# Post-norm decoder layer with experts on one core: the experts' second bias as one float32r product of split rows, the gate weights split by GpSimd

## The reference, cut to what matters

```
def _moe(h, w_gate, we1, be1, we2, be2):      # h: 2048 tokens x 256, E = 4 experts, I = 256
    raw = softmax(x @ w_gate, axis=-1)
    top_vals, top_idx = top_k(raw, 2)
    w = softmax(top_vals, axis=-1)
    comb = zeros((t, E)).at[arange(t)[:, None], top_idx].add(w)
    hmid = gelu(einsum('td,edi->tei', x, we1) + be1[None], approximate=False)
    eout = einsum('tei,eid->ted', hmid, we2) + be2[None]
    out = einsum('te,ted->td', comb, eout)
```

## Time and profile before

| | us |
|---|---|
| median of 3 runs | 1181.89 (1181.88 to 1181.89) |
| the profiled execution, its time | 1185.99 |
| its span | 1184.2 |
| what lies around the span | 1.79 |
| granted TensorE clock, mean | 0.985 of full speed |

### The profile page before, as it was taken

How to read it: one execution, slowest core, us unless ns; L and a number is a source line. 1 busy time by engine, 2 the same in 40 slices (tenths; PEclk the granted TensorE clock), 3 DMA queues, 4 the chain that set the end, 5 groups by cost and what they waited for, 6 DMA issues and landing times.

```text
span 1184.2 us, 30629 instructions
## 1 busy us (share of the span) xinstructions
PE 1116.1 (94%) x11732; PEld 921.1 (78%) x11732; DVE 954.0 (81%) x2219; ACT 667.3 (56%) x1703; POOL 660.2 (56%) x714
## 2 busy tenths in 40 slices
PE   6899999899999999888999999999999999999997
PEld 5667665566666766556899899999999899988887
DVE  6758886877888878867788888888898888878977
ACT  5466564577777777664555544444444444558663
POOL 4457564654545556264778554544544455737665
PEclk9889999989999999989999999999999999999999
DMA  5975544344444444402121000000000100101111
GB/s 162 211 183 131 130 122 110 99 122 120 120 135 135 117 126 119 121 22 86 58 72 55 2 1 1 1 1 1 1 1 1 37 2 1 37 19 36 37 37 36
DMA packets 107490, 83.05 MB, mean 70 GB/s; under 512 B 74171, under 2 KB 95803, under 8 KB 107345
## 3 DMA queue, kind: packets, MB, share of 16 engines
q1 hardware_dynamic: 107345, 81.10, 25.0%
HBM read 57.02 MB, written 23.07 MB: 68 GB/s over the span
## 4 chain that ended last, share of the span: by engine, by line
PE 55%; DVE 14%; issue 6%; POOL 4%; ACT 2%; SPq 1%; DMA 1%; POOLq 0%; DVEq 0%; ACTq 0%
PE bank L1637 5%; PE bank L1638 5%; PE bank L1639 5%; PE bank L1693 4%; PE bank L1666 4%; PE bank L665 3%; PE bank L643 3%; PE bank L562 3%; PE bank L1653 2%; PE bank L1708 2%; PE bank L1706 2%; PE bank L1707 2%; DVE B_nr L808 2%; PE bank L1654 2%; PE bank L1655 2%
## 5 line engine op out<-in xcount | busy, mean ns | idle before, releaser
L1941 POOL TENSOR_TENSOR C_QK<-C_t1b,C_t2b 128x512 f32<-128x512 f32 x128 | 168.7, 1318 | 227.4 <-DVE C_t2b L1780 226.8
L1777 DVE SCALAR_TENSOR_TENSOR C_t1b<-bank,C_bcol,C_tabs 64x512 f32<-64x512 f32 x256 | 192.1, 750 | 38.6 <-PE bank L1639 34.5
L1067 ACT ACTIVATE PT<-bank 128x512 f32<-128x512 f32 x224 | 130.0, 596 | 98.5 <-PE bank L643 96.7
L808 DVE TENSOR_REDUCE B_nr<-bank 128x4 f32<-128x512 f32 x256 | 164.2, 683 | 25.4 <-PE bank L604 25.1
L1637 PE MATMUL bank<-C_XTh,C_Wh 128*128 128x512 f32 x256 | 112.4, 439 | 5.7 <-DVE C_XTl L1626 1.9
L1873 ACT ACTIVATE C_P<-bank,C_nm 128x128 f32<-128x128 f32 x256 | 90.5, 366 | 34.1 <-DVE C_nm L1790 32.4
L1892 ACT ACTIVATE C_V<-bank 128x512 f32<-128x512 f32 x64 | 38.0, 596 | 124.1 <-PE bank L1655 122.6
L1638 PE MATMUL bank<-C_XTl,C_Wh 128*128 128x512 f32 x256 | 101.6, 397 | 0.0
L1639 PE MATMUL bank<-C_XTh,C_Wl 128*128 128x512 f32 x256 | 101.2, 395 | 0.0
L665 PE MATMUL bank<-PT,vpool 128*32 128x128 f32 x2048 | 97.6, 287 | 2.0 <-ACT OTf L1077 2.0
L1780 DVE SCALAR_TENSOR_TENSOR C_t2b<-bank,C_bcol,C_tabs 128x512 f32<-128x512 f32 x128 | 96.1, 751 | 1.8
(11 more groups left out here) (271 smaller groups left out, 3495.0 us busy)
## 6 DMA issues: line engine op xcount, KB each, us to landing
Adrq<-PB SPq DMA_DIRECT2D x16, 192.0 KB, 2.9
Adrk<-PB SPq DMA_DIRECT2D x16, 192.0 KB, 3.1
stk<-Adrq SPq DMA_DIRECT2D x16, 192.0 KB
stk<-Adrk SPq DMA_DIRECT2D x16, 192.0 KB
Bdrq<-PB SPq DMA_DIRECT2D x16, 192.0 KB, 3.0
stk<-Bdrq SPq DMA_DIRECT2D x32, 96.0 KB
Bdrk<-PB SPq DMA_DIRECT2D x16, 192.0 KB, 2.8
stk<-Bdrk SPq DMA_DIRECT2D x32, 96.0 KB
```

The costliest lines, as they stand in the source:

```text
L808: e.tensor_reduce(dst, bank[n % 2][:, :].rearrange("p (a b) -> p a b", a=4), AX.X, ALU.max, negate=True).then_inc(sem("m_dve"), 1)
L1067: e.activation(pt_of(n)[:, :], bank2(n)[:, :], ACT.Exp).then_inc(sem("e_act"), 1)
L1777: e.scalar_tensor_tensor(out=v4(t1b[kq][lo:lo + 64, :]), in0=v4(o[hi:hi + 64, :]), scalar=bc[hi:hi + 64, :], in1=tabsC[hi:hi + 64, 2 * kq ...
L1941: e.tensor_tensor(QK[v % 3][:, kq, :], t1b[kq][:, :], t2b[kq][:, :], ALU.add).then_inc(sem("rc_pool"), 1)
```

## The change

The bias product becomes a float32r product. To keep its precision the operands are split, and the parts lie at different partitions of the same product: in comb128 the columns 0 to 15 and 16 to 31 (through a view of two runs of 64, k = 2, of which the first 16 columns are taken: columns 0 to 15 and 64 to 79) get the weights as float32r, and columns 32 to 47 get what is left of them. In b2, three copies of the rows lie at partitions 0, 32 and 64. ScalarE copies b2 to the float32r tile b2r once (bias_act), and VectorE subtracts that from b2 in partitions 64 to 95 once (bias_dve), so that these hold the low part. One product then sums high x high (partitions 0 on), low weights x high bias (32 on) and high weights x low bias (64 on).

GpSimd does the splitting of the weights (comb_pool): it zeroes the tile in the first two chunks, copies the weights twice as float32r, and subtracts. It stands ahead of residual(0, 0) for chunk 0, and ahead of the last part's hidden_pool (m = 7) for chunks 1 to 3. VectorE writes the weights into a tile of their own (D_combS); its zeroing instruction goes. TensorE's transposition now waits for GpSimd's semaphore comb_zero, and no longer for VectorE's gate_dve.

```diff
+    b2r = sb("D_b2r", [128, 4, 256], F32R, st_d)
...
-    comb = [T[:, 0:16].rearrange("p (a b) -> p a b", a=4) for T in comb128]
-    combT = [sb(f"D_combT{i}", [128, 128], F32, st_d) for i in range(2)]
+    comb = [sb(f"D_combS{i}", [128, 4, 4], F32, st_d) for i in range(2)]
+    combT = [sb(f"D_combT{i}", [128, 128], F32R, st_d) for i in range(2)]
...
     def comb_t_pe(e, q, c):
-        q.wait_ge("gate_dve", 18 * (c + 1))
+        q.wait_ge("comb_zero", min(c, 1) + 1 + 2 * (c + 1))
...
-            q.wait_ge("ld_b2", 16)
+            q.wait_ge("ld_b2", 18)
...
-                    e.matmul(ebank(c, b, x)[:, 256:512], combT[i][:, :], b2[:, b, :], start=True, stop=True)
+                    e.matmul(ebank(c, b, x)[:, 256:512], combT[i][:, :], b2r[:, b, :], start=True, stop=True)
...
-            if c < 2:
-                e.memset(comb128[c][:, :], 0.0).then_inc(sem("comb_zero"), 1)
...
-            q.wait_ge("comb_zero", min(c, 1) + 1)
+            if c >= 2:
+                q.wait_ge("comb_zero", 2 + 2 * (c - 1))
...
+        bias_dve(e, q)
         for c in range(1, NCH):
...
+    def bias_act(e, q):
+        q.wait_ge("ld_b2", 16)
+        e.activation(b2r[:, :, :], b2[:, :, :], ACT.Copy).then_inc(sem("ld_b2"), 1)
+
+    def bias_dve(e, q):
+        low = slice(64, 96)
+        q.wait_ge("ld_b2", 17)
+        e.tensor_tensor(b2r[low, :, :], b2[low, :, :], b2r[low, :, :].bitcast(F32), ALU.subtract).then_inc(sem("ld_b2"), 1)
+
+    def comb_pool(e, q, c):
+        T = comb128[c % 2]
+        if c < 2:
+            e.memset(T[:, :], 0.0).then_inc(sem("comb_zero"), 1)
+        n = min(c, 1) + 1 + 2 * c
+        flat = comb[c % 2][:, :, :].rearrange("p a b -> p (a b)")
+        copies = T[:, :].rearrange("p (k r) -> p k r", k=2)[:, :, 0:16].bitcast(F32R)
+        q.wait_ge("comb_zero", n)
+        q.wait_ge("gate_dve", 18 * (c + 1))
+        if c >= 2:
+            q.wait_ge("ct_pe", c - 1)
+        e.tensor_copy(copies, flat.unsqueeze(1).to_broadcast([128, 2, 16])).then_inc(sem("comb_zero"), 1)
+        q.wait_ge("comb_zero", n + 1)
+        e.tensor_tensor(T[:, 32:48], flat, T[:, 0:16], ALU.subtract).then_inc(sem("comb_zero"), 1)
...
     def act_d(e):
         q = Queue(e, sem)
+        bias_act(e, q)
...
         LAST = (3, 5, 6, 7)
+        comb_pool(e, q, 0)
         residual(0, 0)
         for c in range(1, NCH):
             for m in range(8):
...
+                if m == 7:
+                    comb_pool(e, q, c)
                 hidden_pool(e, q, c, m)
...
     for b in range(4):
-        f["Db2"][4 * b:4 * b + 4, b, :] = g("be2").reshape(4, 256)
+        for k in range(3):
+            f["Db2"][32 * k + 4 * b:32 * k + 4 * b + 4, b, :] = g("be2").reshape(4, 256)
```

## The result

The changed kernel takes 1189.34 us (median of 6 runs, 1187.66 to 1192.03); the kernel before, run beside it, 1181.89 us (6 runs, 1180.90 to 1183.80). The ratio is 1.0057, 95% interval 1.0039 to 1.0074: slower by some 6.7 us (4.6 to 8.7). The forecast was 1186.0 (4.15 us slower), in a range from 1183.8 to 1188.2. The direction came true and the time lies outside the range. The profiled execution took 1190.62, its span 1188.8 us, with a mean granted clock of 0.984.

What follows compares the result with a forecast made beforehand. VectorE was taken to set the pace from 1086.53 to about 1135, TensorE from 1137.17 to 1150.24, then VectorE, then a chain begun by GpSimd. 2.9 + 1.65 - 0.6 + 0.2 = 4.15 us on 1181.89 gave 1186.0, range 1183.8 to 1188.2.

Steps and rivals of the forecast that it cites:

- the first stall: Chunk 0's transposition waits for GpSimd's three splitting instructions and starts at 1086.35; TensorE has nothing to do for 3.9 us.
- the price at full clock: VectorE's first L2201 starts at 1089.45 instead of 1086.53, 2.9 us late, if TensorE's clock stays up.
- TensorE's saving: Sixteen bias products each 0.31 us cheaper, 5.0 us in all; only 0.6 counts, from chunk 2's first two.
- the 3.09 of the forecast: Time in us from chunk 0's transposition to VectorE's L2201: 3.74 less a 0.34 wait and 0.31 of cheaper bias product.
- the rival on the faster side: VectorE's two-operand gate instructions run free of GpSimd in 3 chunks, giving 6.6 us: 1179.4, chance 0.05.
- the prediction's signs of being wrong: L2201 starting before 1089, VectorE gaps between there and 1140, or TensorE waiting for GpSimd in chunks 1 and 2.
- VectorE's own queue: Ahead of chunk 0's first combine, subtracting b2 delays the statistics to 1089.0, 2.5 us late; covered by TensorE's lateness.
- the first slow stretch: Behind chunk 0's stall, some 3.3 us at 1.2 GHz; TensorE gets 1.65 us less done, VectorE starts 4.6 us late.
- The next block is not worse off: The block behind chunk 0's first gets no further delay, having 0.31 us of its own cheaper bias product.
- The term that was put at 4.55 - 0.6: The 2.9 us stall delay plus 1.65 of half clock, less 0.6 gained by chunk 2's cheaper products.
- The second slow stretch: Rival: the clock also falls at the 3 us stall ahead of the last chunk, about 1.5 later: 1187.5, chance 0.28.
- in place of 0.2: Last chunk at full clock: GpSimd's late splitting makes L2349 end at about 1170.3, 0.2 us late.

Runs made afterwards that it cites:

- chunk 0's splitting earlier: The changed kernel with GpSimd's splitting of chunk 0's gate weights moved ahead of that chunk's last low part: 1185.95 us, ratio to before 1.0015.
- stalls filled: The changed kernel with products that nobody reads ahead of the waiting transposition in chunks 0 and 3: 1185.20 us, ratio to before 1.0009.
- the stall alone: The kernel before, with chunk 0's transposition also waiting for GpSimd's first residual: 1187.28 us, ratio to before 1.0027.
- best version: The changed kernel with the splitting earlier in chunks 0 and 3 and the b2 copy and subtraction moved into stage C: 1183.10 us, ratio to before 0.9995.
- the kernel before with the filled stall: The kernel before, chunk 0's transposition also waiting for GpSimd's first residual, with 13 products that nobody reads ahead of the waits: 1183.74 us, one run.
- both earlier: The changed kernel with GpSimd's splitting moved ahead of the last low part in chunk 0 and ahead of part 6 in the last chunk: 1183.70 us, ratio 1.0001.

## Why the prediction was right or wrong

**Right: the place and the size of the first stall.** Forecast: the transposition 1086.35 - 1082.56 = 3.79 us behind the weights, with a gap of 3.9. Measured: 3.91 and 3.92. What hides in it: zeroing and subtraction take 0.21 and 0.22 us, and the copy 0.21 where GpSimd is alone (chunk 0's splitting earlier), less than the 0.3 and 0.25 that were taken; and VectorE's subtraction of b2, which runs at the time, stretches the copy to 0.94. Forecast was that GpSimd's last instruction waits until VectorE is done; it was the copy, which ends at 1084.59, just behind VectorE's end at 1084.52. Two small errors cancelled: the three alone take 0.64 instead of 0.8 us, and the hold-up was 0.73 instead of 0.4.

**Right: the price at full clock.** 2.9 us forecast; 2.88 with the stalls filled.

**Right: VectorE paces, TensorE's saving is worth 0.6 of 5.0.** Between the 1st and the 12th combine nothing is caught up (the stall alone shows it). The product's gain there: 0.94 - 0.30 = 0.64 us behind the first combine in the best version with and without it, and 0.70 between the 1st and the 12th in the run with filled stalls against before. The 0.30 that it gives ahead of the first combine was in the 3.09 of the forecast. Chunks 1 and 2 cost nothing. Nor did VectorE's two-operand instructions give anything on balance, as the rival on the faster side had it: from the 1st to the 9th combine it took 56.60 us, before 56.71. In the experts the group of the earlier trace rows that took 1322 ns takes 955 (L2164 now), the one that took 225 takes 552 (L2170), and the two nearly cancel. One of the prediction's signs of being wrong did come, gaps of VectorE ahead of 1140 (0.18 us at 1092.27, 1.75 at 1097.57), but not what it was to mean, that TensorE's 5.0 us would count.

**Right, but sized too large: VectorE's own queue.** 2.5 us late was forecast, 1.98 measured when nothing else was late. As forecast, it was covered in the changed kernel.

**Wrong: the length of the first slow stretch.** The step is "So the stall of 3.9 us should be followed by a stretch of some 3.3 us at 1.2 GHz". It rested on one stall of 1.64 us. Behind 3.92 us the stretch was 6.7 us long. The trace of the kernel before had other stalls and other lengths, which the prediction didn't use. TensorE's row behind one of them, and windows of two slow stretches (columns as in the earlier trace rows):

```profile
59.42 0.61 PE L643 MATMUL bank<-stk 99*128 99x128 bf16 x4 [2.81 <-DMA stk<-A_nmT]
```

```profile
59.00:65.70 6.70, 6.28 (x42) 3.93 (x43) 0.87 (x2) 2.69 (x5) 3.79 (x4) 0.50 0.84 227
233.10:243.20 10.10, 9.81 (x113) 5.99 (x114) 4.70 (x8) 5.23 (x11) 2.38 (x3) 0.50 0.33 106
```

So 6.7 us, and even 10.1, could have been read before anything was built. Two things followed from the longer stretch. The first combine came 2.15 us later than at full clock instead of 1.65, since TensorE was slow all the way to it and not for the first 3.3 us only. And "The next block is not worse off" fell: at 1097.57 VectorE waited 1.75 us for TensorE a second time, and this block is 16.53 us behind the weights, before 11.14 (1093.70): 5.39 late. Ahead of it VectorE had won 1.5 us (its four C_XN, L1584, took 1.80 us, before 3.33; that they ran against fewer instructions of GpSimd is the likely reason, and wasn't tested); it spent them waiting. What this second wait cost was small: 5.39 against 5.03, and gone by the 9th combine (4.92 late). The term that was put at 4.55 - 0.6 measured 5.03 - 0.42 at the 12th combine: 0.66 us of the miss.

**Wrong: the choice between one slow stretch and two.** The step is "Against it: TensorE is busy without a gap on both sides of it". The stall of the last chunk was forecast at 3 us and measured at 2.92, and the row at 526.57 showed half clock behind a much shorter one. The second slow stretch was given 0.28 with that argument, where ahead of 526.57 TensorE is busy for half the time only the earlier trace rows. The row was right and the conclusion not: nothing showed that a busy TensorE ahead of a stall protects it, and it didn't. The tail took 12.99 instead of 11.42 us: 1.57, where the rival said 1.5 in place of 0.2. With the rival's 1187.5 and the 0.66 us above, the sum comes to 1188.2; by the anchors it is 1181.89 + 6.15 = 1188.04. The true case was the rival. The forecast's size rested on these two steps: of the 6.15 us, 2.15 + 1.50 are half clock by the run with filled stalls, and the sum had 1.65.

**Too narrow: the base.** The remaining 1.3 us, from 1188.04 to the median 1189.34, has no cause in the change that a trace shows, and it needs none: the 6.15 us lie inside the interval of the ratio, 4.6 to 8.7 us, and the forecast's 4.15 just outside it. The runs of the changed kernel spread over 4.4 us, those of the kernel before, over three sets of runs, from 1178.8 to 1187.38, with medians of 1181.89, 1183.89 and 1182.91. The three runs shown, 1181.88 to 1181.89, were alike by chance, and the range took no share for that; nor did the 4.10 us between the profiled execution and their median warn enough. The median lies 1.1 us above the range, which is less than this spread. What the forecast had wrong is therefore better read from the two steps above than from the 1.1 us.

**The bound of the clock.** The upper end of the range, 1188.2, was two slow stretches of 3.3 us. A slow stretch of twice that length had no place in it, though the trace of the kernel before held two longer ones: the rows chosen had a single stall with a slow stretch behind it, the one of 1.64 us.

## What to carry to other kernels

A stall of TensorE on the path can cost its length and then a stretch at half clock: here 2.47 us for the stall of 3.19 and 1.48 for the slow stretch behind it, and in the changed kernel 2.88 and 2.15. Price both, look through the whole trace for stalls and for the lengths of the slow stretches, not at one, and keep the case without a slow stretch as a rival. Where a stall can't be removed, products that nobody reads can keep the clock: they gave back 3.9 of the 6.15 us. When an operand's preparation moves to another engine, look first at what stands in that engine's queue ahead of it and who waits at the far end: here three small instructions, behind a low part and beside VectorE's subtraction, held TensorE for 3.9 us, where alone they take 0.64. And a saving of 5 us on an engine that isn't the one waited for was worth 0.94 in the best version, 0.6 of it behind the first combine; that could be read from the gaps ahead of VectorE's rows before anything was built.

## What was not expected of the hardware

In the experts the slow stretches came in two lengths. 3.3 us: behind stalls of 2.32 (the changed kernel with the float32 product, last chunk), 2.91, 2.92 and 3.19 us, and behind the pair of 0.88 and 1.53. 6.7 us: behind 3.92, and in the changed kernel with the float32 product behind 3.91 (1087.7 to 1094.4, slow). But the length of the stall doesn't decide it. In the first half, in the kernel before, 3.3 us came behind 1.64 and 6.7 us behind 2.81 (59.42, shown above). In the kernel before with the filled stall 3.3 us came behind 3.87, and behind 2.29 at 523.24 the clock stayed up. Rows and windows of the latter kernel:

```profile
30.19 0.58 PE L496 MATMUL bank<-A_Wh,XTh 128*128 128x256 f32 x1 [3.87 <-DVE XTl L794]
523.24 0.47 PE L1637 MATMUL bank<-C_XTh,C_Wh 128*128 128x512 f32 x1 [2.29 <-issue]
```

```profile
30.30:33.60 3.30, 3.30 (x17) 2.66 (x18) 0.84 (x2) 0.58 (x2) 0.95 (x2) 0.50 0.85 217
523.30:526.60 3.30, 3.30 (x52) 2.23 (x52) 2.15 (x5) 0.79 (x2) 0.53 (x1) 1.00 0.03 7
```

Whether a short stall is followed by one at all is not fixed by the program: with the same instructions, and stalls equal to 0.01 us, the clock fell in one profile and stayed in another (chunk 0's splitting earlier, both earlier). What decides stays open; it wasn't tried.

The same shows in the first 550 us, where no kernel here differs. This stretch in the kernel before and in the kernel before with the filled stall (columns as in the earlier trace rows):

```profile
0.00:550.00 550.00, 498.64 (x7424) 353.54 (x7425) 424.77 (x868) 353.96 (x855) 294.01 (x403) 0.97 0.47 125
```

```profile
0.00:550.00 550.00, 494.86 (x7464) 352.90 (x7464) 429.99 (x877) 353.44 (x855) 298.07 (x406) 0.99 0.47 125
```

In finer windows of these 550 us the half clock makes up 34.0 us in the one and 10.2 in the other (27.2 in the changed kernel, 20.4 with its stalls filled), and the weights of chunk 0 come at 1082.56 and 1077.81. So the clock in the loosely filled first half is likely a part of the spread of whole runs. It is not all of it: four profiles have 20.4 us of half clock there (stalls filled, chunk 0's splitting earlier, both earlier, and the best version with the float32 product), and their weights come at 1081.10, 1078.38, 1077.41 and 1076.24. A comparison of stretches from an anchor inside the changed part tells differences of 0.3 us that the medians can't: the tail, where nothing delays it, took 11.42 or 11.43 us in six profiles. The Trainium skill, "TensorE: Matmul & The Clock Gate", Part 1, says that the number of slow products at a kernel's start differs between runs of one kernel; these traces agree, and show it far behind the start too, with 10.2 to 34.0 us of half clock in the first 550 us.

VectorE and GpSimd hold each other up also where one of the two instructions is tiny: the copy of 128x32 took 0.94 us beside VectorE's subtraction and 0.21 alone, and ended 0.07 us behind it. The zeroing, which reads no tile, took its 0.21 us (1083.38) inside the same subtraction without being held up. The subtraction itself, begun beside GpSimd's low part, took 1.45 us; where it began first, 1.22 (1062.51), it was GpSimd's instruction that waited (it took 2.07 us, its like mostly 1.04). The Trainium skill, "SBUF — State Buffer", section "SBUF: two separate sides", has the loser wait for the whole instruction of the other; the copy's rows agree.
